# Tridiagonalization: the guard under the norm's square root moves from a TensorE product to the bias operand of ScalarE's root

## The chip, the cores and the metric

The kernel runs on one core of a Trainium2 chip, in one launch. The metric is device time in microseconds (us) for the whole launch, of which the changed stage is one part. PE is TensorE (PEld its weight loads), DVE is VectorE, ACT is ScalarE.

## The reference, cut to what matters

The model is a chain of graph and feed-forward layers on x (16 x 512 x 128). One of the graph layers needs all eigenvectors of a normalized 512 x 512 Laplacian:

```python
deg = jnp.sum(A, axis=0) + jnp.sum(A, axis=1) - jnp.diagonal(A)
d_inv_sqrt = jnp.where(deg > 0, jax.lax.rsqrt(deg), 0.0)
L = jnp.diag(deg) - A
L_norm = d_inv_sqrt[:, None] * L * d_inv_sqrt[None, :]
_, U = jnp.linalg.eigh(L_norm)
agg = jnp.einsum('mn,bnd->bmd', U.T, features)
```

The kernel finds U by first bringing L_norm to tridiagonal form with Householder reflections, one for each of 512 columns. A reflection needs the norm of the remaining column, so a square root of a sum of squares. Where that sum is zero, the reciprocal of the root must still be finite: this is what the guard, the constant TINY = 2^-100, is for.

## The kernel before

`tridiagonalize` is the first stage of the program. It walks the 512 columns in four phases of 128 steps; in phase `ph` only the lower 4 - ph blocks of 128 rows are live, so phase 0 has the most work for TensorE (48 small products `ax` per step) and phase 3 the least (3). A phase has eight panels of 16 steps (`PW = 16`), numbered j = 0 to 15. Within a panel the corrections by earlier steps of the same panel are carried along (`VW`, `prod`, `sums`, `sr`), so DVE's work in a step grows with j. At the end of a panel the trailing matrix is updated.

The order on each engine is written out by hand, and the engines signal each other with semaphores. One step runs like this (line numbers of the kernel before):

- DVE forms the sums per partition: the square of the column (L309) and its first element (L311), and signals `part_in`. It goes on with preparations: L314 to L320 split the vector for the bf16 products, L323 and L329 make the corrections' sums `sums`.
- PE adds these over the 128 partitions by a product with a matrix of ones: `tot[q][:, 0:2]` (L456). Then it makes part of the `ax` products (L471), the product of the corrections' sums `sr` (L460) and the rest of `ax`.
- ACT waits for `tot` and takes the root (L432), signalling `root_out`; then it prepares the next step's masks (L172, L174).
- DVE waits for the root and takes its reciprocal (L333), refines the norm (L338), makes c (L343), multiplies the corrections with `sr` (L347, which waits for L460), sums them (L353), and combines them with `ax` (L363, which waits for L471; ahead of it in phases 1 to 3, behind it in phase 0, stands the reciprocal L372).
- After two more sums over partitions, PE makes the product `dots` (L476). ACT scales the vector (L436) and stores it (L438, L439). DVE finishes the next step's column with `dots` (L400, L403) and the next step's L309 follows.

The guard: `tiny` holds TINY / 128 in each partition. A product of ones with `tiny` (L477) opens the accumulation of the next step's `tot` bank with TINY (`start=True, stop=False`), and L456 of that step adds to it (`start=False`). `tot` has two banks, used in turn; before the first step L451 opens the first one, and after the last L492 closes the one that nobody uses. A product of 32-bit numbers is carried out in two passes, so each of these lines has two weight loads and two matmul records.

Of the kernel before, what the change touches and what calls it, by code (L numbers as in the profile page):

```python
# [10 lines left out]
ACT = mybir.ActivationFunctionType  # L11
AX = mybir.AxisListType
P = 128
N = 512
NB = N // P
# [60 lines left out]
def tridiagonalize(nc, C, adj_d, adjT_d, V, G, ER, DR, also):  # L76
# [10 lines left out]
    with ExitStack() as ctx:  # L87
        def sb(name, shape, dt=F32):
            return ctx.enter_context(nc.sbuf_tensor("h_" + name, shape, dt))
# [3 lines left out]
        def sem(name):  # L93
            return signal("h_" + name)
# [31 lines left out]
        part = sb("part", [P, 4])  # L126
        zy = sb("zy", [P, 2, NB])
        s = sb("s", [P, 16])
        TINY = 2.0 ** -100
        tiny = sb("tiny", [P, 2])  # L130
        T1, T2 = sb("T1", [PAIR, N]), sb("T2", [PAIR, N])
        M = ctx.enter_context(nc.psum_tensor("h_M", [P, NB, N], F32))
        bcast = M[:, 0, :]
# [1 line left out]
        tot = [ctx.enter_context(nc.psum_tensor("h_tot%d" % q, [P, N], F32)) for q in range(2)]  # L135
        sr = ctx.enter_context(nc.psum_tensor("h_sr", [P, N], F32))
        turned, dots = M[0:PAIR, NB - 2, :], M[:, 0, 0:2]
        loaded, made, ch, also_in = sem("loaded"), sem("masks_made"), sem("chain"), sem("also_in")
        root_in, root_out = sem("root_in"), sem("root_out")
        diag_in, row_out, row_sb = sem("diag_in"), sem("row_out"), sem("row_sb")  # L140
        ax_out = sem("ax_out")
        part_in, tot_out, dots_out = sem("part_in"), sem("tot_out"), sem("dots_out")
# [33 lines left out]
        with nc.Block() as block:  # L176
# [8 lines left out]
            @block.gpsimd  # L185
            def _(pool):
                nc.gpsimd.memset(eye[:, :, :], 0.0).then_inc(made, 1)
                nc.gpsimd.memset(masks[:, :, :, :], 0.0).then_inc(made, 1)
                nc.gpsimd.memset(A[:, :, N:EDGE], 0.0).then_inc(made, 1)
                nc.gpsimd.memset(tiny[:, :], TINY / P).then_inc(made, 1)  # L190
                nc.gpsimd.memset(prod2[:, :, :, :, :], 0.0).then_inc(made, 1)
                pool.wait_ge(made, 5)

                nc.gpsimd.affine_select(out=eye[:, :, :], in_=eye[:, :, :], compare_op=ALU.not_equal, fill=1.0, base=0,
                                        pattern=[[P, NB], [-1, N]], channel_multiplier=1).then_inc(made, 1)
                nc.gpsimd.affine_select(out=masks[:, :, 0, :], in_=masks[:, :, 0, :], compare_op=ALU.not_equal, fill=1.0,
                                        base=-1, pattern=[[P, NB], [-1, EDGE]], channel_multiplier=1).then_inc(made, 1)

                for m, off in ((1, 1),):
                    nc.gpsimd.affine_select(out=masks[:, :, m, :], in_=masks[:, :, m, :], compare_op=ALU.is_ge, fill=1.0,  # L200
                                            base=off, pattern=[[-P, NB], [1, EDGE]],
                                            channel_multiplier=-1).then_inc(made, 1)
# [83 lines left out]
        for ph in range(NB):  # L286
            L, c0 = NB - ph, ph * P
            live = slice(ph, NB)
            with nc.Block() as block:
# [132 lines left out]
                @block.scalar  # L422
                def _(act):
                    if ph == 0:
                        nc.scalar.activation(root[:, :], dis[:, :], ACT.Sqrt).then_inc(loaded, 1)
                        act.wait_ge(loaded, 33)
                        next_step(act, 0, live, 0)
                    for panel in range(ph * P // PW, (ph + 1) * P // PW):
                        for j in range(PW):
                            k, q, J = panel * PW + j, j % 2, 2 * j  # L430
                            act.wait_ge(tot_out, j + 1)
                            nc.scalar.activation(s[:, 5:6], tot[q][:, 0:1], ACT.Sqrt).then_inc(root_out, 1)  # L432
                            if j < PW - 1:
                                next_step(act, 1 - q, live, k + 1)
                            act.wait_ge(scaled_in, j + 1)
                            nc.scalar.activation(VW[:, live, J:PAIR + J + 2:PAIR + 1], v[:, live].unsqueeze(2).broadcast_to([P, L, 2]),  # L436
                                                 ACT.Copy, scale=s[:, 9:10]).then_inc(scaled_out, 1)
                            nc.scalar.activation(CVG[:, ds(k, 1), :].rearrange("p o t -> p (o t)"), s[:, 7:10], ACT.Copy)  # L438
                            nc.scalar.activation(V[:, live, ds(k, 1)].rearrange("p b o -> p (b o)"), v[:, live], ACT.Copy).then_inc(kept, 1)  # L439
                        act.wait_ge(turn2_out, 1)  # L440
                        act.sem_clear(turn2_out)
                        act.sem_clear(scaled_in)
                        act.sem_clear(tot_out)
                        nc.scalar.activation(T2[:, c0:], M[0:PAIR, NB - 1, c0:], ACT.Copy).then_inc(turn_sb, 1)
                        split_parts(act, ph)
                        next_step(act, 0, live, panel * PW + PW)

                @block.tensor
                def _(pe):
                    if ph == 0:  # L450
                        nc.tensor.matmul(tot[0][:, 0:2], C.ones[:, :], tiny[:, :], start=True, stop=False)  # L451
                    for panel in range(ph * P // PW, (ph + 1) * P // PW):
                        for j in range(PW):
                            q = j % 2
                            pe.wait_ge(part_in, 2 * j + 1)
                            nc.tensor.matmul(tot[q][:, 0:2], C.ones[:, :], part[:, 0:2], start=False, stop=True).then_inc(tot_out, 1)  # L456

                            def corrections():
                                pe.wait_ge(sums_in, j + 1)
                                nc.tensor.matmul(sr[:, 0:1 + 4 * j], C.ones[:, :], sums[:, 0:1 + 4 * j], start=True, stop=True).then_inc(sr_out, 1)  # L460

                            pe.wait_ge(xb_in, j + 1)
                            if j == 0:
                                pe.wait_ge(parts_ready, L)
                                pe.sem_clear(parts_ready)
                            for m in range(ph, NB):
                                if m == (ph + 1 if L > 2 else ph):
                                    corrections()
                                for b in range(ph, NB):
                                    for n, A_part in enumerate(parts):  # L470
                                        ins = nc.tensor.matmul(ax[:, m, 0:3], A_part[:, b, m * P:(m + 1) * P],  # L471
                                                               XB[:, q, b, 2 * XC + 1:2 * R2 + 2:2],
                                                               start=(b == ph and n == 0), stop=(b == NB - 1 and n == 2))
                            ins.then_inc(ax_out, 1)
                            pe.wait_ge(part_in, 2 * j + 2)
                            nc.tensor.matmul(dots, C.ones[:, :], part[:, 2:4], start=True, stop=True).then_inc(dots_out, 1)  # L476
                            nc.tensor.matmul(tot[1 - q][:, 0:2], C.ones[:, :], tiny[:, :], start=True, stop=False)  # L477
                        pe.wait_ge(panel_in, 1)
                        for used in (panel_in, part_in, sums_in, xb_in):
                            pe.sem_clear(used)  # L480
                        for t, out, signalled in ((0, turned, turn_out), (1, M[0:PAIR, NB - 1, :], turn2_out)):
                            for b in range(ph, NB):
                                ins = nc.tensor.transpose(out[:, b * P:(b + 1) * P],
                                                          VW[:, b, t * PAIR:(t + 1) * PAIR], C.ident[:, :])
                            ins.then_inc(signalled, 1)
                        pe.wait_ge(turn_sb, 2)
                        pe.sem_clear(turn_sb)
                        for b in range(ph, NB):
                            nc.tensor.matmul(M[:, b, c0:], T1[:, b * P:(b + 1) * P], T2[:, c0:], start=True,
                                             stop=True).then_inc(upd_out, 1)  # L490
                    if ph == NB - 1:
                        nc.tensor.matmul(tot[0][:, 0:2], C.ones[:, :], tiny[:, :], start=False, stop=True)  # L492

        with nc.Block() as block:
            @block.vector
# [2728 lines left out]
```

## Time and profile before

| what | value |
|---|---|
| median of 3 runs | 7038.33 us (7036.03 to 7038.71) |
| span of the profiled execution | 7032.6 us, from its first to its last instruction |
| the tridiagonalization's steps in it | from 45 to 2509 us |
| PE busy over the span | 5280.7 us (75%), 33091 matmul records |
| DVE busy | 4595.9 us (65%) |
| ACT busy | 2313.6 us (33%) |
| records of L477 | 1024 weight loads, 1024 matmuls: two of each in each of 512 steps |

The time of the profiled execution is its span and what lies around it; only the span is on record, and the median of the runs is 5.7 us above it. Busy shares are averages over stages that differ widely: what a change to this stage is worth has to be read from the stage itself, at the point where one engine waits for another.

### The profile page before, as it was taken

The page shows a single profiled execution, that of the slowest core. Times are in us where ns is not written, and L with a number is a line of the kernel's source. Part 1 is how long each engine was busy: PE and PEld are TensorE (multiplying, and loading weights), DVE is VectorE, ACT ScalarE, POOL GpSimd, SP SyncE. Part 2 cuts the span into 40 slices and gives each one's busy share as a digit, 9 for nine tenths or more (in the row PEclk, how much of TensorE's full clock was granted, in tenths as well). Part 3 has the DMA queues.
Part 4 walks back from the last instruction along what each step waited for, and adds up shares of the span by engine and source line. Part 5 has one row for each costly group of instructions (what it writes and reads, how often), then busy time and mean ns, then how long its engine had stood idle before and what let it go on. Part 6 is the DMA issues. An engine that isn't in the chain of part 4 may idle for free. (4 is left out here: it accounts for less than half of the span.)

```text
span 7032.6 us, 110639 instructions
## 1 busy us (share of the span) xinstructions
PE 5280.7 (75%) x33091; PEld 3792.1 (54%) x33091; DVE 4595.9 (65%) x27972; ACT 2313.6 (33%) x7361; POOL 17.9 (0%) x36
## 2 busy tenths in 40 slices
PE   5777666655555569988999995895574699876899
PEld 4666555555544435545666663563342467544676
DVE  7888888887878753337999999678444333424333
ACT  2222222222222224336778985110020133301333
POOL 0000000000000000000000000000000000000000
PEclk9999999999999999988999997997787799976899
DMA  0000000000000000000000000000010000000000
GB/s 37 2 2 2 2 1 1 1 1 1 1 1 1 1 20 1 0 35 19 6 4 6 6 4 8 1 1 1 1 48 1 12 0 0 9 0 13 0 0 24
DMA packets 23221, 48.24 MB, mean 7 GB/s; under 512 B 5673, under 2 KB 16322, under 8 KB 20930
## 3 DMA queue, kind: packets, MB, share of 16 engines
q1 hardware_dynamic: 22722, 42.40, 1.8%
q8 instruction: 213, 3.49, 0.2%
q14 instruction: 286, 2.34, 0.1%
HBM read 34.00 MB, written 8.39 MB: 6 GB/s over the span
## 5 line engine op out<-in xcount | busy, mean ns | idle before, releaser
L476 PE MATMUL h_M<-h_part,ones 128*128 128x2 f32 x1024 | 300.5, 363 | 576.2 <-DVE h_jd L384 576.2
L476 PEld LDWEIGHTS h_M<-h_part,ones 128*128 128x128 f32 x1024 | 256.4, 311 | 619.9 <-DVE h_jd L384 619.9
L1774 DVE SCALAR_TENSOR_TENSOR f_ACC<-f_yp,f_CG,f_ACC 128x128 f32<-128x128 f32 x1024 | 288.2, 344 | 461.8 <-DVEq L1772 461.8
L1719 PEld LDWEIGHTS f_yp<-f_W,f_hs 128*128 128x128 f32 x4096 | 490.1, 192 | 92.6 <-issue 91.8
L1653 PE MATMUL f_hp<-f_rows,f_W 128*128 128x512 f32 x1024 | 531.5, 601 | 5.1 <-ACT U L1663 3.1
L821 ACT ACTIVATE e_XD<-e_X,e_scal 128x60 f32<-128x60 f32 x2048 | 527.7, 333 | 17.5 <-DVEq L685 15.7
L1750 ACT ACTIVATE f_hs<-f_hp,f_b 128x512 f32<-128x512 f32 x512 | 347.6, 685 | 539.7 <-ACTq L1749 539.7
L471 PEld LDWEIGHTS h_ax<-h_XM,h_parts 128*128 128x128 bf16 x11520 | 508.8, 116 | 0.0
L1709 PE MATMUL f_hp<-f_XT,f_W 128*128 x1024 | 483.7, 600 | 33.0 <-PEq L2003 33.0
L436 ACT ACTIVATE h_VW<-h_v,h_s 128x8 f32<-128x8 f32 (+3 forms) x512 | 154.9, 302 | 1044.6 <-DVE h_s L388 1044.6
L1719 PE MATMUL f_yp<-f_W,f_hs 128*128 128x128 f32 x4096 | 493.5, 275 | 0.0
L456 PE MATMUL h_tot<-h_part,ones 128*128 128x2 f32 x1024 | 300.3, 363 | 227.8 <-DVE h_jb L311 227.8
L471 PE MATMUL h_ax<-h_XM,h_parts 128*128 128x3 bf16 x11520 | 425.5, 167 | 0.0
L456 PEld LDWEIGHTS h_tot<-h_part,ones 128*128 128x128 f32 x1024 | 256.3, 311 | 298.9 <-DVE h_jb L311 298.9
L1643 PEld LDWEIGHTS f_yp<-f_W,UT 128*128 128x128 f32 x2048 | 266.5, 194 | 188.8 <-issue 92.2
L460 PE MATMUL h_sr<-h_sums,ones 128*128 128x1 f32 (+15 forms) x1024 | 314.9, 397 | 48.4 <-DVE h_sums L329 34.5
L1643 PEld LDWEIGHTS f_yp<-f_W,U 128*128 128x128 f32 x2048 | 268.6, 192 | 114.2 <-issue 93.2
L432 ACT ACTIVATE h_s<-h_tot 128x1 f32<-128x1 f32 x512 | 87.6, 171 | 696.9 <-PE h_tot L456 696.9
L1643 PE MATMUL f_yp<-f_W,UT 128*128 128x128 f32 x2048 | 281.0, 281 | 41.4 <-ACT UT L1663 32.2
L460 PEld LDWEIGHTS h_sr<-h_sums,ones 128*128 128x128 f32 x1024 | 257.4, 312 | 71.6 <-issue 44.8
L477 PE MATMUL h_tot<-h_tiny,ones 128*128 128x2 f32 x1024 | 289.7, 353 | 0.0
L2340 PE MATMUL g_PG<-g_HL,g_Wih 128*128 128x256 f32 (+2 forms) x624 | 288.5, 619 | 0.6 <-DVE g_HL L2287 0.6
(688 smaller groups left out, 11242.6 us busy)
## 6 DMA issues: line engine op xcount, KB each, us to landing
f_S<-in_f_W SPq DMA_DIRECT2D x64, 128.0 KB, 2.4
X<-in_x SPq DMA_DIRECT2D x1, 4096.0 KB, 16.3
f_W<-in_f_W SPq DMA_DIRECT2D x2, 2048.0 KB
spill<-f_xts SPq DMA_DIRECT2D x16, 256.0 KB, 2.0
f_rows<-spill SPq DMA_DIRECT2D x16, 256.0 KB, 2.6
f_W<-in_f_W SPq DMA_DIRECT2D x4, 1024.0 KB
out<-X SPq DMA_DIRECT2D x1, 4096.0 KB, 11.1
h_A<-in_adj SPq DMA_DIRECT2D x1, 1024.0 KB, 5.4
```

What stands on the lines that cost most here:

```text
L456: nc.tensor.matmul(tot[q][:, 0:2], C.ones[:, :], part[:, 0:2], start=False, stop=True).then_inc(tot_out, 1)
L460: nc.tensor.matmul(sr[:, 0:1 + 4 * j], C.ones[:, :], sums[:, 0:1 + 4 * j], start=True, stop=True).then_inc(sr_out, 1)
L471: ins = nc.tensor.matmul(ax[:, m, 0:3], A_part[:, b, m * P:(m + 1) * P], XB[:, q, b, 2 * XC + 1:2 * R2 + 2:2], start=(b == ph and n == 0), ...
L476: nc.tensor.matmul(dots, C.ones[:, :], part[:, 2:4], start=True, stop=True).then_inc(dots_out, 1)
L477: nc.tensor.matmul(tot[1 - q][:, 0:2], C.ones[:, :], tiny[:, :], start=True, stop=False)
L821: ins = nc.scalar.activation(XD[b][:, k, h, :], X[:, :], ACT.Identity, bias=scal[b][:, k, 2 * h:2 * h + 1])
L1643: ins = nc.tensor.matmul(self.yp[d % 3][:, 0:D], self.hs[unit % 2][:, j, i * P:(i + 1) * P], self.W2[:, unit % E * FC + j, :], start=(j == ...
L1653: nc.tensor.matmul(self.hp[s % 3][:, :], self.W1[:, e, j * P:(j + 1) * P], self.rows[:, g % 2, :], start=True, stop=True).then_inc(self.h_ ...
L1709: nc.tensor.matmul(hp[:, u % 2, c, :], W1[:, col // F, col % F:col % F + P], rows_t, start=True, stop=True).then_inc(h_full, 1)
L1719: ins = nc.tensor.matmul(yp[:, u % 2, k, :], hs[:, u % 2, c, k * P:(k + 1) * P], W2[:, u * UC + c, :], start=(c == 0), stop=(c == UC - 1))
L1750: nc.scalar.activation(hs[:, u % 2, c, :], hp[:, u % 2, c, :], func, bias=b1[:, u * UC + c:u * UC + c + 1]).then_inc(hs_full, 1)
L2340: ins = nc.tensor.matmul(o2, Wih[:, p - 1, gi * D:(gi + 1) * D], x, start=True, stop=(t == 0))
```

## The change

The guard is no longer summed by TensorE. `tiny` holds TINY itself, one column, and is handed to the root as its bias, so that ACT takes the root of `tot + tiny`. The products L451, L477 and L492 are gone, and L456 opens and closes its bank alone. `tot` is now the bare sum of squares; L338, which reads it too, sees it without TINY.

```diff
-        tiny = sb("tiny", [P, 2])
+        tiny = sb("tiny", [P, 1])
...
-                nc.gpsimd.memset(tiny[:, :], TINY / P).then_inc(made, 1)
+                nc.gpsimd.memset(tiny[:, :], TINY).then_inc(made, 1)
...
-                            nc.scalar.activation(s[:, 5:6], tot[q][:, 0:1], ACT.Sqrt).then_inc(root_out, 1)
+                            nc.scalar.activation(s[:, 5:6], tot[q][:, 0:1], ACT.Sqrt, bias=tiny[:, 0:1]).then_inc(root_out, 1)
...
-                    if ph == 0:
-                        nc.tensor.matmul(tot[0][:, 0:2], C.ones[:, :], tiny[:, :], start=True, stop=False)
...
-                            nc.tensor.matmul(tot[q][:, 0:2], C.ones[:, :], part[:, 0:2], start=False, stop=True).then_inc(tot_out, 1)
+                            nc.tensor.matmul(tot[q][:, 0:2], C.ones[:, :], part[:, 0:2], start=True, stop=True).then_inc(tot_out, 1)
...
-                            nc.tensor.matmul(tot[1 - q][:, 0:2], C.ones[:, :], tiny[:, :], start=True, stop=False)
...
-                    if ph == NB - 1:
-                        nc.tensor.matmul(tot[0][:, 0:2], C.ones[:, :], tiny[:, :], start=False, stop=True)
```

PE's rows at the first two steps of phase 0, before (h_tot is the bank of the sums, h_sr the corrections, h_M the bank that holds `dots`):

```order
L451 MATMUL h_tot<-h_tiny,ones 128x2
L456 MATMUL h_tot<-h_part,ones 128x2
L465 ISA
L471 MATMUL h_ax<-h_XM,h_parts 128x3 x12
L460 MATMUL h_sr<-h_sums,ones 128x1
L471 MATMUL h_ax<-h_XM,h_parts 128x3 x36
L476 MATMUL h_M<-h_part,ones 128x2
L477 MATMUL h_tot<-h_tiny,ones 128x2
L456 MATMUL h_tot<-h_part,ones 128x2
L471 MATMUL h_ax<-h_XM,h_parts 128x3 x12
```

The same place after the change, where the lines of PE's code have moved up by two:

```order
L454 MATMUL h_tot<-h_part,ones 128x2
L463 ISA
L469 MATMUL h_ax<-h_XM,h_parts 128x3 x12
L458 MATMUL h_sr<-h_sums,ones 128x1
L469 MATMUL h_ax<-h_XM,h_parts 128x3 x36
L474 MATMUL h_M<-h_part,ones 128x2
L454 MATMUL h_tot<-h_part,ones 128x2
L469 MATMUL h_ax<-h_XM,h_parts 128x3 x12
```

Between the product of `dots` and the next step's sum of squares nothing stands any more; the rest of PE's order is as it was.

ACT's rows around the first step's root, before:

```order
L172 ACTIVATE h_XM<-h_masks 128x4x2
L174 ACTIVATE h_prod2<-h_A 128x4
L432 ACTIVATE h_s<-h_tot0 128x1
L172 ACTIVATE h_XM<-h_masks 128x4x2
L174 ACTIVATE h_prod2<-h_A 128x4
L436 ACTIVATE h_VW<-h_v,h_s 128x4x2
```

And after:

```order
L172 ACTIVATE h_XM<-h_masks 128x4x2
L174 ACTIVATE h_prod2<-h_A 128x4
L432 ACTIVATE h_s<-h_tot0,h_tiny 128x1
L172 ACTIVATE h_XM<-h_masks 128x4x2
L174 ACTIVATE h_prod2<-h_A 128x4
L436 ACTIVATE h_VW<-h_v,h_s 128x4x2
```

The order is the same; the root reads a second operand, one number per partition from memory, where its bias was a constant inside the instruction. DVE's order is unchanged.

## Rows read from the trace of the kernel before

**Rows 1.** The page: span.

```profile
span 7032.6 us, 110639 instructions
```

**Rows 2.** Busy time by stretch (phase 3; a later stretch), with PEclk.

```profile
core 0: us, PE busy (x) PEld busy (x) DVE busy (x) ACT busy (x) POOL busy (x), PEclk, DMA share, GB/s
...
1958.90:2509.40 550.50, 299.96 (x1440) 265.15 (x1440) 440.51 (x4357) 113.61 (x788) 0.00 (x0) 1.00 0.00 1
3122.00:3207.00 85.00, 46.01 (x202) 42.06 (x203) 48.84 (x162) 13.02 (x21) 1.94 (x2) 0.50 0.26 100
```

**Rows 3.** Groups by line, whole span: busy us, mean ns, idle before, releasers.

```profile
L456 PE MATMUL h_tot<-h_part,ones 128*128 128x2 f32 x1024 | 300.3, 363 | 227.8 <-DVE h_jb L311 227.8
L477 PEld LDWEIGHTS h_tot<-h_tiny,ones 128*128 128x128 f32 x1024 | 280.0, 333 | 0.0
...
L432 ACT ACTIVATE h_s<-h_tot 128x1 f32<-128x1 f32 x512 | 87.6, 171 | 696.9 <-PE h_tot L456 696.9
...
L333 DVE RECIPROCAL h_s<-h_s 128x1 f32<-128x1 f32 x512 | 83.2, 162 | 101.3 <-ACT h_s L432 90.7
```

**Rows 4.** Weight loads by line in the second stretch of rows 2.

```profile
L1610 PEld LDWEIGHTS f_lp<-f_Wr,f_xts 128*128 128x128 f32 x128 | 29.1, 333 | 0.0
```

**Rows 5.** Timeline, phase 3, step j = 5: start us, duration us, [idle before].

```profile
2047.72 0.59 PE L456 MATMUL h_tot<-h_part,ones 128*128 128x2 f32 x2 [0.25 <-DVE h_jb L311]
...
2048.34 0.17 ACT L432 ACTIVATE h_s<-h_tot 128x1 f32<-128x1 f32 x1 [1.36 <-PE h_tot L456]
...
2048.55 0.16 DVE L333 RECIPROCAL h_s<-h_s 128x1 f32<-128x1 f32 x1 [0.29 <-ACT h_s L432]
...
2049.07 0.16 DVE L343 TENSOR_TENSOR h_s<-h_s 128x1 f32<-128x1 f32 x1
2049.15 0.17 DVE L347 TENSOR_TENSOR h_prod<-h_VW,h_sr 128x20 f32<-128x20 f32 x1
...
2050.45 0.59 PE L476 MATMUL h_M<-h_part,ones 128*128 128x2 f32 x2 [1.40 <-DVE h_jd L384]
...
2051.15 0.23 DVE L400 SCALAR_TENSOR_TENSOR h_XM<-h_vm,h_M,h_base 128x1 f32<-128x1 f32 x1 [0.22 <-PE h_M L476]
```

**Rows 6.** Timeline of DVE, phase 3, the panel's last step, j = 15.

```profile
2089.59 0.16 DVE L343 TENSOR_TENSOR h_s<-h_s 128x1 f32<-128x1 f32 x1
2089.75 0.22 DVE L347 TENSOR_TENSOR h_prod<-h_VW,h_sr 128x60 f32<-128x60 f32 x1
```

**Rows 7.** Timeline of DVE, phase 2, step j = 12.

```profile
1498.90 0.16 DVE L343 TENSOR_TENSOR h_s<-h_s 128x1 f32<-128x1 f32 x1
1499.04 0.25 DVE L347 TENSOR_TENSOR h_prod<-h_VW,h_sr 128x96 f32<-128x96 f32 x1
```

**Rows 8.** Timeline of DVE, phase 1, step j = 12.

```profile
878.67 0.16 DVE L343 TENSOR_TENSOR h_s<-h_s 128x1 f32<-128x1 f32 x1
878.85 0.30 DVE L347 TENSOR_TENSOR h_prod<-h_VW,h_sr 128x144 f32<-128x144 f32 x1
```

**Rows 9.** Timeline of PE and DVE, phase 0, step j = 8.

```profile
169.55 0.64 PE L460 MATMUL h_sr<-h_sums,ones 128*128 128x33 f32 x2
170.00 0.75 PE L471 MATMUL h_ax<-h_XM,h_parts 128*128 128x3 bf16 x22
...
170.02 0.16 DVE L343 TENSOR_TENSOR h_s<-h_s 128x1 f32<-128x1 f32 x1
170.23 0.29 DVE L347 TENSOR_TENSOR h_prod<-h_VW,h_sr 128x128 f32<-128x128 f32 x1
```

**Rows 10.** Timeline of DVE, phase 0, step j = 3.

```profile
148.60 0.16 DVE L372 RECIPROCAL h_s<-h_s 128x2 f32<-128x2 f32 x1
148.81 0.17 DVE L363 TENSOR_REDUCE h_y<-h_ax 128x4 f32<-128x12 f32 x1
```

**Rows 11.** ACT's groups by line and form, whole span.

```profile
L1750 ACT ACTIVATE f_hs<-f_hp,f_b 128x512 f32<-128x512 f32 x512 | 347.6, 685 | 539.7 <-ACTq L1749 539.7
...
L436 ACT ACTIVATE h_VW<-h_v,h_s 128x2 f32<-128x2 f32 x128 | 38.1, 297 | 236.8 <-DVE h_s L388 236.8
...
L172 ACT ACTIVATE h_XM<-h_masks 128x2 f32<-128x2 f32 x128 | 25.3, 197 | 0.0
...
L2359 ACT ACTIVATE g_G<-g_PG 128x512 f32<-128x512 f32 x16 | 9.6, 597 | 54.3 <-PE g_PG L2301 54.3
```

## The prediction

> **What bounds the kernel now.** The change touches only the 512 steps of the tridiagonalization, so I read this stage and leave the page's shares of the whole span [rows 1] aside. First question: does anything wait for the product that goes? In the groups by line, L456, the next instruction on PE behind L477, found PE idle 227.8 us in total, 0.44 us in each of 512 steps, and every bit of it was put down to DVE's L311 [rows 3]. In the timeline of a step PE stands idle 0.25 us after L477's second pass until L311 signals [rows 5]. L477 has run out before the next sum of squares is asked for.
>
> Second question: does anything wait for the root, which gets a second operand? ACT sat idle 696.9 us, 1.36 us a step, until L456 released it, and DVE's L333 sat idle 90.7 us until L432 released it [rows 3]. In the step of phase 3 the order is plain: L456 begins at 2047.72, the root begins at 2048.34, is over at 2048.51, and L333 begins at 2048.55, 0.29 us after DVE had run out of work [rows 5]. PE to ACT to DVE is a chain with nothing beside it in such a step, and DVE then works on almost without a stop to the step's end. So DVE's order with this round trip in it bounds the stage, not PE.
>
> **The change part by part.**
>
> *L477, L451 and L492 go.* The weight loads of L477 alone take PE 280.0 us, but PE is idle behind each product until DVE's signal comes [rows 3, 5]. The cover is that idle time, and it stays. Worth: nothing. If L456 could start with L477 gone, it would only wait longer for the same L311.
>
> *L456 opens its bank itself.* Passes of L476, which opens and closes its own, take together 0.59 us after a 1.40 us pause, and those of L456, which adds to an open bank after 0.25 us, 0.59 us too [rows 5]. Worth: nothing, in spite of the longer pause.
>
> *TensorE's clock.* Less work for PE could bring a lower clock. The windows print 1.00 for phase 3, yet its 32-bit weight load takes 333 ns, exactly what L1610's takes in a stretch with a granted 0.50 [rows 2 to 4]. I take it that the stage already runs at the lower of the two levels (1.2 GHz), so this can cost nothing more.
>
> *The root reads its bias from memory.* The trace has no root with such an operand. The nearest rows: from the matmul banks to memory, 128x512, a copy without one takes 597 ns (L2359) and L1750 with a bias per partition 685 ns: 88 ns more. From memory to memory, 128x2, L172 without takes 197 ns and L436 with a scale per partition 297 ns: 100 ns more [rows 11]. Below, the price could be nothing only if the operand were fetched while ACT waits; L436 had waited 236.8/128 = 1.85 us before each execution and still paid [rows 11]. I take 88 ns, since L1750 has the root's kind of source and a bias rather than a scale: the root goes from 171 to 259 ns. The range keeps 88 to 100.
>
> The Trainium skill, "ScalarE: Activation LUTs", section "What ACT_TABLE_LOAD costs", speaks against this change: each operand of one number per partition adds about 93 ns to an ACTIVATE with immediate scale and bias. By that the estimated sum below would be 26.0 us instead of 24.4. No row shows a root with such an operand; the two differences above stand on either side of the skill's figure.
>
> *Who is late next.* L333 starts 88 ns later wherever it waits for the root, and all of DVE behind it with it, until DVE meets another wait that is later anyway. Two DVE instructions that wait for nothing begin 0.08 us apart, as L343 and L347 [rows 5]; a larger distance is spare time, used to cover the delay. The first place is L347, which waits for PE's product L460. That product depends on L329, not on the root, and comes later as j grows.
>
> - Phase 3: no spare time at steps 0 to 10 (0.08 us between L343 and L347), so 11 x 88 = 968 ns a panel pass. From step 11 to the last, the distance grows to 0.16 [rows 6], spare 0, 20, 40, 70, 90 ns by the timeline, so some 85, 65, 45, 18 and 0 are left: 213. Together 1181 ns a panel.
> - Phase 2: free of waits at steps 0 to 9, 880 ns. Then 0.02 us more a step, 0.14 at step 12 [rows 7]: 71, 45, 25, 4, 0, 0 are left, 145. Together 1025.
> - Phase 1: at step 0 L363 waits for `ax` and covers all; steps 1 to 8 pass 704; step 9 71, step 10 46, step 11 5; by step 12 the distance is 0.18, spare 0.10, and covers all [rows 8]. Together 826.
> - Phase 0: hardly anything. Early steps have L363 waiting for `ax`, which doesn't depend on the root: at step 3, L363 begins 0.21 us after L372, spare 0.13 [rows 10]. Late steps have L347 waiting for L460: at step 8 the distance is 0.21, spare 0.13 [rows 9]. Between, the two covers together take nearly all; about 20 ns a panel.
>
> Further on, L400 waits for PE's answer to L384, and L384 moves with the rest, so nothing is absorbed there. ACT's L172 and L174 behind the root are 88 ns later too, but the next step is what needs them, over 2 us on. Eight panels a phase: 8 x (1181 + 1025 + 826 + 20) = 24.4 us. At 100 ns the same arithmetic gives 28.5 us.
>
> **The sum.** The span goes from 7032.6 to 7057.0 us; with the 5.7 us that the runs' median lies above it, 7062.7, say 7063 us: 0.35% slower.
>
> **Rivals.**
>
> 1. *The bias costs nothing (the other side).* It is fetched while ACT waits for L456, the root stays at 171 ns, and L477 is hidden: 7038 us, no change. For it: the address is known and ACT idles 1.36 us [rows 5]. Against: L436 idles longer and pays [rows 11]. It decides if the root grows by less than some 54 ns, since by the same subtraction of spare times that makes 14 us, the 0.2% that a measurement of this kernel can tell from no change.
> 2. *L477 holds up the answer to `dots` (faster).* L400 begins 0.11 us after L476's last pass ends (2051.04 to 2051.15), while the root begins 0.03 after L456's [rows 5]. If L477, right behind, were the cause, its removal would give 0.08 x 512 = 41 us against the 24 of the bias: 7021 us. Against: L460 also has products right behind it, and L347 begins 0.04 after its end (170.19 to 170.23) [rows 9]; L400 has a second operand to wait for, which is a likelier reason.
> 3. *Nothing absorbs.* If the waits at L347 and L363 move with DVE, all 512 steps pay: 512 x 88 = 45 us, 7083 us. Against: L460 and L471 need sums and parts that DVE makes ahead of L333.
>
> **How the numbers follow.** The forecast, part of the steps paying 88 to 100 ns: chance 0.84. Rival 1: 0.07. Rival 3, or halfway to it: 0.05. Rival 2: 0.03; its counterweight of less than the whole 41 us would end near no change, 0.01. The likeliest case's own range is 7060 (24.4 with the runs' spread of 2 us below) to 7069 (28.5 and the spread above). For 8 times in 10 I give 7057 to 7070, with a little on the low side for spare times read to 10 ns only. Slower by over 0.2% (7052.4) takes the forecast and rival 3: 0.89; within 0.2%: 0.08; faster: 0.03.
>
> **What the profile after would show.** L432 at about 259 ns (right), 171 (rival 1). L333's idle time put down to ACT grows by 88 ns in each step that waited, so by some 30 us or more, as steps that hardly waited now do. L347's and L363's waits in phase 0 shrink by about as much. Phase 0 lasts as long as before; phases 1, 2 and 3 are longer by some 6.6, 8.2 and 9.4 us. PE's idle time before the sum of squares grows by about L477's time, and nobody gains. L400 still begins 0.11 us after its product. The forecast is wrong if the root's price is far from 88 ns, if phase 0 grows by several us, or if later stages move, which nothing here touches.

## The result and the profile after

The changed kernel takes 7057.6 us (median of 8 runs, 7051.58 to 7060.2) against 7040.0 us before (8 runs, 7036.03 to 7044.4): a ratio of 1.0025, 95% interval [1.0016, 1.0034]. It is slower by a quarter of a per cent, 17.6 us. A second comparison on another occasion gave 1.0021 [1.0012, 1.0030].

The page of the changed kernel, its span and busy times:

```profile
span 7049.2 us, 108583 instructions
...
PE 5052.8 (72%) x32063; PEld 3565.2 (51%) x32063; DVE 4587.6 (65%) x27972; ACT 2360.2 (33%) x7361; POOL 17.9 (0%) x36
```

PE has 1028 matmuls less and 228 us less to do, ACT has 47 us more, and the kernel is slower. The groups by line that answer to [rows 3] (L454 is L456 of before):

```profile
L454 PE MATMUL h_tot<-h_part,ones 128*128 128x2 f32 x1024 | 300.1, 363 | 449.4 <-DVE h_jb L311 449.4
...
L432 ACT ACTIVATE h_s<-h_tot,h_tiny 128x1 f32<-128x1 f32 x512 | 133.7, 261 | 697.2 <-PE h_tot L454 697.2
...
L333 DVE RECIPROCAL h_s<-h_s 128x1 f32<-128x1 f32 x512 | 83.5, 163 | 142.6 <-ACT h_s L432 137.3
```

PE's idle time before the sum of squares doubled, from 227.8 to 449.4 us: what the product gave up became idle time of the engine that had it. The product itself takes 363 ns a pass as before. The root went from 171 to 261 ns, and DVE's idle time put down to it from 90.7 to 137.3 us.

The step of [rows 5] in the timeline of the changed kernel (start us, duration us, idle before):

```profile
2064.00 0.59 PE L454 MATMUL h_tot<-h_part,ones 128*128 128x2 f32 x2 [0.68 <-DVE h_jb L311]
...
2064.62 0.26 ACT L432 ACTIVATE h_s<-h_tot,h_tiny 128x1 f32<-128x1 f32 x1 [1.36 <-PE h_tot L454]
...
2064.92 0.16 DVE L333 RECIPROCAL h_s<-h_s 128x1 f32<-128x1 f32 x1 [0.38 <-ACT h_s L432]
...
2065.45 0.16 DVE L343 TENSOR_TENSOR h_s<-h_s 128x1 f32<-128x1 f32 x1
2065.52 0.17 DVE L347 TENSOR_TENSOR h_prod<-h_VW,h_sr 128x20 f32<-128x20 f32 x1
...
2066.82 0.58 PE L474 MATMUL h_M<-h_part,ones 128*128 128x2 f32 x2 [1.49 <-DVE h_jd L384]
...
2067.51 0.23 DVE L400 SCALAR_TENSOR_TENSOR h_XM<-h_vm,h_M,h_base 128x1 f32<-128x1 f32 x1 [0.22 <-PE h_M L474]
```

From the sum of squares to the root's start it takes 0.62 us as before; L333 follows 0.30 after the root's start, where it was 0.21; everything behind it has kept its distance. L400 still begins 0.11 after its product's end (2067.40), though nothing stands behind that product now.

How long the steps take is best read from L309, the first instruction of each step: its first and last start, of before and of the changed kernel.

```profile
L309 DVE SCALAR_TENSOR_TENSOR h_ja<-h_XM x512: 150/155/165, 45.0 to 2502.6; 128x4 f32<-128x4 f32 x43, 128x3 f32<-128x3 f32 x43, 128x1 f32<-128x1 f32 x43, 128x2 f32<-128x2 f32 x42
```

```profile
L309 DVE SCALAR_TENSOR_TENSOR h_ja<-h_XM x512: 150/155/166, 45.0 to 2527.0; 128x4 f32<-128x4 f32 x43, 128x3 f32<-128x3 f32 x43, 128x1 f32<-128x1 f32 x43, 128x2 f32<-128x2 f32 x42
```

That is 2457.6 and 2482.0 us: the steps are 24.3 us longer. By phase, from the starts of L309 at its first step to the next phase's (for phase 3, to the last step):

| phase | before, us | after, us | difference | predicted |
|---|---|---|---|---|
| 0 | 703.78 | 703.88 | 0.1 | 0.2 |
| 1 | 626.16 | 633.06 | 6.9 | 6.6 |
| 2 | 584.18 | 591.83 | 7.7 | 8.2 |
| 3 | 543.51 | 553.20 | 9.7 | 9.4 |

But the span grew by 16.6 us only, and the median by 17.6. About 7 us of the loss were given back behind the last step, in stages that the change doesn't touch. So there are two questions: is the root's operand the cause of the 24 us, and where do the 7 us come from?

### The profile page after: what moved, and what is told of

It reads as the page before. It is cut to its first block and busy times, and to the rows that moved or that the text cites. A ratio compares the mean times of both kernels' runs of the same rounds, so it can differ in the third digit from the quotient of the medians.

```text
span 7049.2 us, 108583 instructions
## 1 busy us (share of the span) xinstructions
PE 5052.8 (72%) x32063; PEld 3565.2 (51%) x32063; DVE 4587.6 (65%) x27972; ACT 2360.2 (33%) x7361; POOL 17.9 (0%) x36
## 5 line engine op out<-in xcount | busy, mean ns | idle before, releaser
L454 PE MATMUL h_tot<-h_part,ones 128*128 128x2 f32 x1024 | 300.1, 363 | 449.4 <-DVE h_jb L311 449.4
L816 ACT ACTIVATE e_XD<-e_X,e_scal 128x60 f32<-128x60 f32 x2048 | 527.6, 333 | 17.6 <-DVEq L680 15.7
L454 PEld LDWEIGHTS h_tot<-h_part,ones 128*128 128x128 f32 x1024 | 256.0, 310 | 521.9 <-DVE h_jb L311 521.9
L432 ACT ACTIVATE h_s<-h_tot,h_tiny 128x1 f32<-128x1 f32 x512 | 133.7, 261 | 697.2 <-PE h_tot L454 697.2
L701 DVE SCALAR_TENSOR_TENSOR e_PB<-e_PB,e_scal,e_u 128x60 f32<-128x60 f32 x1024 | 278.6, 272 | 0.0
```

The lines of the kernel that those rows point to most:

```text
L816: ins = nc.scalar.activation(XD[b][:, k, h, :], X[:, :], ACT.Identity, bias=scal[b][:, k, 2 * h:2 * h + 1])
```

## The experiments

Theory A: the whole loss is the operand that the root reads from memory, and the removed product was free. Theory B, its rival: the loss comes from PE, whose sum of squares now starts after a longer pause and opens its own bank. Theories C to E are about the later stages: C, they gain because the product is gone; D, they only scatter; E, they take one of several courses by the instant at which they begin. Differences below are against the runs of the kernel before in the same comparison, those of the steps against its profile.

**e1_imm: the guard as a constant in the instruction.** The changed kernel with one edit:

```diff
-   nc.scalar.activation(s[:, 5:6], tot[q][:, 0:1], ACT.Sqrt, bias=tiny[:, 0:1]).then_inc(root_out, 1)
+   nc.scalar.activation(s[:, 5:6], tot[q][:, 0:1], ACT.Sqrt, bias=TINY).then_inc(root_out, 1)
```

> The guard is given to the root as a constant inside the instruction (TINY itself), no product with tiny, no operand from memory. Theory A (the loss is the operand read from memory, the removed product was free): root back at 171 ns, the 512 steps from the first to the last L309 take 2457.6 us as before (within 1 us), not 2482.0; total within 0.15% of the kernel before, 7035 to 7045 us. Theory B (the loss comes from PE: the sum of squares after a longer pause, or opening its own bank): steps about 2482 us although the root is at 171 ns. Theory C (later stages gain about 8 us because fewer PE instructions stand in the program): steps as under A, total about 8 us below the kernel before.

Its rows, by line and for L309:

```profile
L454 PE MATMUL h_tot<-h_part,ones 128*128 128x2 f32 x1024 | 300.3, 363 | 449.1 <-DVE h_jb L311 449.1
...
L432 ACT ACTIVATE h_s<-h_tot 128x1 f32<-128x1 f32 x512 | 87.6, 171 | 696.3 <-PE h_tot L454 696.3
```

```profile
L309 DVE SCALAR_TENSOR_TENSOR h_ja<-h_XM x512: 149/154/166, 45.0 to 2501.5; 128x4 f32<-128x4 f32 x43, 128x3 f32<-128x3 f32 x43, 128x1 f32<-128x1 f32 x43, 128x2 f32<-128x2 f32 x42
```

PE pauses as long as in the changed kernel (449.1 us), yet the steps take 2456.5 us, 1.2 us less than before. Theory B falls. The product's removal by itself is worth 1.2 us in this profile, nearly all of it in phase 2 (583.22 against 584.18 us). The total is 7031.5 us against 7037.3, a ratio of 0.9993 [0.9984, 1.0002].

**e2_ptr: the operand alone.** The kernel before with its product, and a bias of zero from memory:

```diff
-   nc.scalar.activation(s[:, 5:6], tot[q][:, 0:1], ACT.Sqrt).then_inc(root_out, 1)
+   nc.scalar.activation(s[:, 5:6], tot[q][:, 0:1], ACT.Sqrt, bias=C.zero[:, 0:1]).then_inc(root_out, 1)
```

> The kernel before, with its product of ones and tiny, and a bias of zero read from memory by the root. Theory A: root 261 ns, steps 2481 to 2483 us (24 to 25 us more), total 18 to 25 us above the kernel before. Theory B: steps 2457.6 us, no change. Theory C: as A in the steps, but without the gain of later stages, so total the full 24 us above.

```profile
L309 DVE SCALAR_TENSOR_TENSOR h_ja<-h_XM x512: 150/155/166, 45.0 to 2527.8; 128x4 f32<-128x4 f32 x43, 128x3 f32<-128x3 f32 x43, 128x1 f32<-128x1 f32 x43, 128x2 f32<-128x2 f32 x42
...
L432 ACT ACTIVATE h_s<-h_tot,zero 128x1 f32<-128x1 f32 x512 | 134.1, 262 | 697.2 <-PE h_tot L456 697.2
```

The root took 262 ns and the steps 2482.8 us, 25.2 more than before. The total is 7065.1 us, 27.8 above the median before; the ratio is 1.0038 [1.0024, 1.0052]. So the operand alone makes the whole loss in the steps, with PE as it was. Against the changed kernel the later stages gave nothing back.

**e3_two: a second operand from memory.** The changed kernel, with its scale of 1.0 read from memory as well:

```diff
-   ... ACT.Sqrt, bias=tiny[:, 0:1]).then_inc(root_out, 1)
+   ... ACT.Sqrt, bias=tiny[:, 0:1], scale=C.ones[:, 0:1]).then_inc(root_out, 1)
```

> The changed kernel, whose root reads its scale (1.0) from memory too. Theory A with spare times as read from the trace before: root about 351 ns (180 more than before); in phase 3 the whole delay passes in nearly all steps, phase 0 still nearly none; sum over the steps 60 us (3.8, 16.2, 19.3 and 21.2 by phase), steps about 2518 us. If nothing is absorbed: 512 x 0.18 = 92 us, steps 2550. If the second operand is read together with the first, root 261 ns and steps 2482 us.

The groups by line, and L309:

```profile
L432 ACT ACTIVATE h_s<-h_tot,h_tiny,ones 128x1 f32<-128x1 f32 x512 | 179.8, 351 | 697.2 <-PE h_tot L454 697.2
...
L333 DVE RECIPROCAL h_s<-h_s 128x1 f32<-128x1 f32 x512 | 83.7, 163 | 185.3 <-ACT h_s L432 182.0
...
L309 DVE SCALAR_TENSOR_TENSOR h_ja<-h_XM x512: 149/155/166, 45.0 to 2560.9; 128x4 f32<-128x4 f32 x43, 128x3 f32<-128x3 f32 x43, 128x1 f32<-128x1 f32 x43, 128x2 f32<-128x2 f32 x42
```

The root took 351 ns, 180 more than before, so each operand has its own price. The steps took 2515.9 us, 58.3 more, where the spare times of the trace before gave 60 and no absorption would give 92. By phase: 2.7, 16.1, 18.4 and 21.1 us (3.8, 16.2, 19.3, 21.2 expected). The map of who absorbs what holds at twice the delay. The total was 7085.9 us, 1.0065 [1.0046, 1.0084], from four runs between 7072.8 and 7102.9.

**e4_triple and e8_double: what covers the product.** The kernel before with two further products of ones and `tiny` behind L477 in each step, or with one (the guard is then three times or twice as large):

```diff
                             nc.tensor.matmul(tot[1 - q][:, 0:2], C.ones[:, :], tiny[:, :], start=True, stop=False)
+                            for _ in range(2):
+                                nc.tensor.matmul(tot[1 - q][:, 0:2], C.ones[:, :], tiny[:, :], start=False, stop=False)
```

> The kernel before with three products of ones and tiny in place of one in each step (the guard is three times as large). Theory A (one product is free only because PE is idle about 0.3 us behind it): each further product holds PE for 0.43 us, so the sum of squares begins 0.4 to 0.5 us late in every step, and nothing absorbs it: steps 190 to 260 us longer, idle time of PE before L456 near zero. If products with tiny cost nothing in themselves whatever their number: steps 2457.6 us.

> The kernel before with two products of ones and tiny per step (the guard is twice as large). One more product holds PE for 0.43 us and PE is idle 0.25 to 0.28 us in the matmul rows before L456, 0.34 us in the weight loads: either the second just fits, since three made each step 0.33 us longer and each further one costs 0.43 (so 0.33 - 0.43 is below nothing), steps 2458 to 2465 us, or it is late by what is missing, 0.1 to 0.15 us a step, steps 2510 to 2535 us.

L309 with one more product, then with two more:

```profile
L309 DVE SCALAR_TENSOR_TENSOR h_ja<-h_XM x512: 150/155/167, 45.0 to 2505.1; 128x4 f32<-128x4 f32 x43, 128x3 f32<-128x3 f32 x43, 128x1 f32<-128x1 f32 x43, 128x2 f32<-128x2 f32 x42
...
L309 DVE SCALAR_TENSOR_TENSOR h_ja<-h_XM x512: 149/155/167, 45.0 to 2674.2; 128x4 f32<-128x4 f32 x43, 128x3 f32<-128x3 f32 x43, 128x1 f32<-128x1 f32 x43, 128x2 f32<-128x2 f32 x42
```

With one more product the steps took 2460.1 us (+2.5), with two more 2629.2 us (+171.5). There is one run of each, 7036.9 and 7203.8 us in all. PE's rows in the timeline show why; first with one more, a step of phase 3:

```profile
2047.78 0.59 PE L476 MATMUL h_M<-h_part,ones 128*128 128x2 f32 x2 [1.43 <-DVE h_jd L384]
2048.22 0.57 PE L477 MATMUL h_tot<-h_tiny,ones 128*128 128x2 f32 x2
2048.65 0.57 PE L479 MATMUL h_tot<-h_tiny,ones 128*128 128x2 f32 x2
2049.07 0.57 PE L456 MATMUL h_tot<-h_part,ones 128*128 128x2 f32 x2
```

And with two more:

```profile
2176.21 0.59 PE L476 MATMUL h_M<-h_part,ones 128*128 128x2 f32 x2 [1.63 <-DVE h_jd L384]
2176.66 0.56 PE L477 MATMUL h_tot<-h_tiny,ones 128*128 128x2 f32 x2
2177.08 0.99 PE L479 MATMUL h_tot<-h_tiny,ones 128*128 128x2 f32 x4
2177.94 0.56 PE L456 MATMUL h_tot<-h_part,ones 128*128 128x2 f32 x2
```

Each product holds PE for 0.43 us. With one more PE's row is full: the sum of squares starts 1.29 us after `dots` here and 1.30 in the median of phase 3, where it was 1.27 in the kernel before. With two more it is 1.73, so 0.46 later than before. The idle time in front of L456 was room for one more product, but for some 0.03 us, and the one that was removed had cost next to nothing. I expected that nothing would absorb the delay of the two (190 to 260 us in all), and was wrong: phase 3 lost 0.39 us a step, phase 0 only 0.24.

**e5_after_again, e6_imm_again, e7_ptr_again: the later stages.** No new edit; the changed kernel, e1's and e2's side by side.

> The changed kernel once more, beside the next two on one chip. Steps 2482.0 us. If the time outside the steps doesn't depend on the product (theory D: later stages only scatter), its median is 24 us above the kernel before, within 3. If kernels without the product gain in later stages (theory C), it is 15 to 20 us above.

> The constant guard without the product once more. Steps 2456 to 2458 us. Theory D: median within 3 us of the kernel before. Theory C: 5 to 9 us below it.

> The product kept and the bias of zero from memory once more. Steps 2482 to 2483 us. Theories C and D both: median 22 to 28 us above the kernel before, since the product stands.

L309 of e5_after_again and of e7_ptr_again:

```profile
L309 DVE SCALAR_TENSOR_TENSOR h_ja<-h_XM x512: 150/155/166, 45.0 to 2527.2; 128x4 f32<-128x4 f32 x43, 128x3 f32<-128x3 f32 x43, 128x1 f32<-128x1 f32 x43, 128x2 f32<-128x2 f32 x42
...
L309 DVE SCALAR_TENSOR_TENSOR h_ja<-h_XM x512: 150/155/165, 45.0 to 2527.4; 128x4 f32<-128x4 f32 x43, 128x3 f32<-128x3 f32 x43, 128x1 f32<-128x1 f32 x43, 128x2 f32<-128x2 f32 x42
```

The changed kernel: 7046.8 against 7035.6 us before, 11.2 more, with 24.6 more in the steps. The constant guard: 7018.9 us, 16.7 less, ratio 0.9978 [0.9969, 0.9987]. The operand with the product kept: 7062.4 us, 26.8 more. Theory D falls: both kernels without the product finish their later stages earlier, by 13.4 and 15.6 us; the one with it does not. Nor is it the instant alone: e5 and e7 begin their last steps 0.2 us apart, and their medians differ by 15.6 us.

The largest single piece lies in eight short rounds of products late in the kernel, from the first to the last instruction that writes `g_MN`. The windows of that stretch, of the kernel before, then of e6_imm_again (columns as in [rows 2]; the third number from the end is PEclk):

```profile
6301.10:6367.00 65.90, 49.40 (x152) 40.45 (x152) 13.28 (x28) 0.00 (x0) 0.00 (x0) 0.67 0.00 0
```

```profile
6298.50:6343.70 45.20, 28.75 (x152) 24.07 (x152) 13.29 (x28) 0.00 (x0) 0.00 (x0) 1.00 0.00 0
```

The work is the same, 152 matmuls. With TensorE's clock granted in full (2.4 GHz) all through, the stretch takes 45.2 us; where it changes between the two levels, mean 0.67, 65.9. Of the seven profiled executions of kernels without the product, four had the 45.2 us (e1, e5, e6, e12) and the others 61.0 (the first profile after) and 64.3 (e3, e11). The seven with it (the one before, e2, e4, e7 to e10) had 64.3 or 65.9. Between the kernel before and e1 the stretch makes up the whole difference behind the last L309 (4530.0 against 4509.8 us).

Each profile is of one run only. Those of e1, e6 and e12 are the shortest of their kernels' 11 runs and that of e5 the third shortest, so they don't tell how often the short course is taken. Over the runs themselves the time goes with the mean granted clock: in e5 from 7037.6 us at 0.935 to 7063.6 at 0.931.

**e9 to e12: the instant moved.** The kernel before and e1's, with two or six copies of an operation of 0.73 us behind the last step:

```diff
-                for b in range(NB):
+                for b in [0] * 2 + list(range(NB)):
                     nc.vector.scalar_tensor_tensor(junk[:, :], A[:, b, 0:N], 1.0, eye[:, b, :], ALU.mult, ALU.mult,
                                                    accum_out=dis[:, b:b + 1]).then_inc(ch, 1)
```

> The kernel before, with two more copies of an idle DVE operation (0.73 us each, the first of four that are there already) behind the last step, so that all later stages begin 1.5 us later. Theory C (later stages are shorter because the product is gone, 13 to 16 us in the second comparison): 1.5 us above the kernel before, within 3 us. Theory E (later stages take one of several courses of TensorE's granted clock, by the instant at which they begin, and the product's removal only moved that instant): the difference is off 1.5 us by 5 us or more here or in the next kernel.

> The same with six copies, 4.4 us. Theory C: 4.4 us above the kernel before, within 3 us. Theory E: off that by 5 us or more here or in the one ahead.

> The kernel with the constant guard and no product, with two copies, 1.5 us. Theory C: 10 to 16 us below the kernel before, as the one without a delay (16.7 below in the second comparison) and 1.5 us. Theory E: another difference from the kernel before here or in the next, with the stretch of eight short rounds behind the last graph layer (44 us at a steady clock, 59 to 62 at an alternating one) the first to change.

> The same with six copies, 4.4 us. Theory C: 7 to 13 us below the kernel before. Theory E: another difference here or in the one ahead.

| kernel | median against before | less steps and added delay |
|---|---|---|
| e9_before_d2 | +2.5 (1.0004 [0.9995, 1.0013]) | +0.5 |
| e10_before_d6 | +6.2 (1.0009 [1.0000, 1.0018]) | +1.9 |
| e11_imm_d2 | -4.5 (0.9996 [0.9987, 1.0005]) | -5.7 |
| e12_imm_d6 | -0.3 (0.9996 [0.9986, 1.0005]) | -3.7 |

With the product, the delay cost itself and no more, against theory E. Without it, 5.7 and 3.7 us of gain were left, and the medians lie 4.5 and 0.3 us below the kernel before, where theory C asked for 10 to 16 and 7 to 13. That the delay shrank the gain isn't shown: e1 and e6 are the same kernel without any delay, and gave 4.6 and 15.6 us.

In all seven comparisons of kernels without the product the later stages are shorter, by 3.7 to 15.6 us (6.7, 13.4, 4.6, 15.6, 9.7, 5.7, 3.7 for the changed kernel twice, e1, e6, e3, e11, e12); in the four with it they are longer by 0.5 to 2.6. A ratio is known to about 6 us either way (13 in e3, 10 in e2 and e7), so only those of the changed kernel and e6 stand by themselves and the others by their common sign. That the product's absence shortens the later stages is shown by this pattern; the size isn't settled. More products don't lengthen them: behind the last L309 the run of e8 takes 4530.0 us, as the kernel before, and that of e4 4528. By what path PE's work or code in the first stage reaches a stretch 3.8 ms later is open.

## Why the prediction was right, point by point

- **L477 is free.** Right: with it gone and the guard a constant the steps are 0.2 to 1.2 us shorter (e1, e6, e11, e12), and one more costs 2.5 us (e8).
- **L456 after a longer pause, opening its own bank.** Right: 363 ns a pass in the kernel before, the changed one and e1.
- **The root's price.** 88 ns taken, 90 measured, from the row that shared the root's kind of source. The Trainium skill, "ScalarE: Activation LUTs", section "What ACT_TABLE_LOAD costs", states about 93 ns for each such operand; the runs agree within 3 ns, and the second operand of e3 cost 90 ns again.
- **Who absorbs it.** Right in place and size: 24.4 us predicted for the steps, 24.3 measured. It holds step by step, so it is not luck: in phase 3 the first 11 steps of a panel grew by 88 to 94 ns on average and the last five by 78, 54, 38, 27 and 6, where the prediction had 85, 65, 45, 18 and 0. In phase 0 `ax` and the corrections' product cover it: DVE's idle time before L333 grew there by 6.9 us, before L347 and L363 it shrank by 4.7. Spare time is used up where it was read: at phase 3's last step L347 stood 0.16 us behind L343 [rows 6], and stands 0.07 behind it in the changed kernel:

```profile
2106.72 0.16 DVE L343 TENSOR_TENSOR h_s<-h_s 128x1 f32<-128x1 f32 x1
2106.79 0.22 DVE L347 TENSOR_TENSOR h_prod<-h_VW,h_sr 128x60 f32<-128x60 f32 x1
```

- **Rival 1** (no price) fell with the 261 ns. **Rival 2** (the product holds up `dots`) fell with L400, which still begins 0.11 us behind its product. The reason that the prediction held likelier, L400's second operand, doesn't explain the 0.11 us: L397, which makes it, was over at 2050.92 in the kernel before, 0.12 us ahead of the product's end. What takes it is open. **Rival 3** (nothing absorbs) fell in phase 0 and in e3.
- **The later stages.** Here a step failed: "if later stages move, which nothing here touches". They moved, by -6.7 us in the first comparison and -13.4 in the second, so the total was 17.6 and 11.2 us where 24.4 were predicted. The sum carried the rest of the span over unchanged, and the reading of the clock stopped at the steps; but the part of the rest that depends on the granted clock is not constant.
- **The total** came out within the range by luck: 7057.6 us lies 0.6 us above the lower end of 7057 to 7070 and below the likeliest case's own 7060 to 7069, because of a gain that the prediction didn't have. The second comparison's 11.2 us, put on the prediction's 7038 us, would lie outside.

## What to carry to other kernels

An engine's work is worth removing only where somebody waits for it: here about 0.43 us of PE's time a step was free, and 90 ns of ACT's, on the round trip that DVE waits for, were not. A constant that an instruction can carry inside it (e1, e6) costs nothing, where the same constant as an operand from memory costs 90 ns each time. The version with the constant is the fastest of all here, 0.9993 and 0.9978 of the kernel before, the first of which can't be told from no change. To price a delay, follow it from instruction to instruction until a wait that is later anyway takes it in, and do so for each phase of a loop, since the spare time differs from phase to phase.

## What the runs showed of the hardware

The same 152 matmuls took 45.2 us at a steadily granted clock and 61.0 to 65.9 where it changed between its levels, in executions of kernels that don't differ there. It is the largest single difference between the profiles behind the steps. The medians of two kernels with the same later stages and equally long steps, e5 and e7, differ by 15.6 us; that this stretch makes that difference too isn't shown, since only one run of each was profiled.

A second operand from memory costs a root as much as the first: 171, 261 and 351 ns with none, one and two.

At some panel ends of phase 2 the next step begins about 0.16 us earlier without the product: from the last step's L309 of the fourth panel to the next step's it takes 11.20 us in the kernel before, e2, e7, e9 and e10, and 11.03 or 11.04 in the changed kernel, e1, e6, e11 and e12. What delays it is open.
